# Second layer of a two-layer block on one Trainium2 core: score products of a head pair as two 64-row tiles, one exponential and one maximum for the pair, one miscellaneous PSUM bank

## The reference

```
q, k, v = x@Wq+bq, x@Wk+bk, x@Wv+bv        # q, k rotated (RoPE)
attn = softmax(q k^T / sqrt(8))            # 1024 x 1024 per head
x1 = layernorm(x + (attn v) @ Wo + bo)
comb = top-2 of softmax(x1 @ Wg), renormalised          # (1024, 8)
y[e] = gelu(x1 @ W1[e] + b1[e]) @ W2[e] + b2[e]         # all 8 experts
out = layernorm(x1 + sum_e comb[e] * y[e])
```

## Time and profile before

| | |
|---|---|
| median of 3 runs | 3107.3 us (3100.91 to 3108.63) |
| the profiled execution, its span | 3107.4 us |
| PE / DVE / ACT / POOL busy | 1506.1 / 2382.8 / 1370.3 / 173.1 us |
| layer 1 and its norms | 0 to about 1582 us |
| prologue of layer 2 | about 1582 to 1654 us |
| from V of the first pass to V of the next | 222.0 us |
| two full passes (V to V) | 711.1 us |
| tail (last values product to the end) | about 172 us |

### The profile page before, as it was taken

How to read it: one execution, slowest core, us unless ns; L and a number is a source line. 1 busy time by engine, 2 the same in 40 slices (tenths; PEclk the granted TensorE clock), 3 DMA queues, 4 the chain that set the end, 5 groups by cost and what they waited for, 6 DMA issues and landing times. The chain is left out here.

```text
span 3107.4 us, 48199 instructions
## 1 busy us (share of the span) xinstructions
PE 1506.1 (48%) x7936; PEld 733.5 (24%) x8061; DVE 2382.8 (77%) x15872; ACT 1370.3 (44%) x3634; POOL 173.1 (6%) x259
## 2 busy tenths in 40 slices
PE   2001010010100101001029998999889998999697
PEld 1000000000000000000012223444345442445264
DVE  6898988989889898898948886777566765676623
ACT  1233333333333333333524666556665666566532
POOL 3000000000000000000100200110002000110000
PEclk8555555555555555555558999999999999999999
DMA  4000000000000000000061111020200201010100
GB/s 105 1 1 1 1 1 1 1 1 1 1 1 1 1 1 1 1 1 1 2 138 20 52 29 25 1 63 8 43 1 1 63 17 33 1 52 18 25 1 7
DMA packets 59835, 56.63 MB, mean 18 GB/s; under 512 B 6602, under 2 KB 43124, under 8 KB 59488
## 3 DMA queue, kind: packets, MB, share of 16 engines
q1 hardware_dynamic: 59488, 53.20, 7.2%
HBM read 29.98 MB, written 22.54 MB: 17 GB/s over the span
## 5 line engine op out<-in xcount | busy, mean ns | idle before, releaser
L1026 DVE TENSOR_REDUCE nm_half<-s 128x1 f32<-128x512 f32 x1088 | 700.8, 685 | 246.7 <-PE s L1203 208.7
L197 ACT ACTIVATE ex<-row,nmax 128x65 f32<-128x65 f32 x960 | 335.9, 350 | 1005.5 <-DVE nmax L299 856.9
L951 ACT ACTIVATE pt<-s 128x512 f32<-128x512 f32 x1024 | 567.1, 596 | 415.2 <-PE s L1213 402.6
L257 DVE SCALAR_TENSOR_TENSOR junk<-ex,tab 128x65 f32<-128x65 f32 x2850 | 619.6, 218 | 3.4
L360 PE MATMUL p_s<-tab,bdg 128*128 128x32 f32 x120 | 31.9, 406 | 842.6 <-DVE tab L262 842.6
L1213 PE MATMUL s<-qs,ks 128*128 128x512 bf16 x949 | 361.8, 388 | 76.2 <-ACT pt L951 60.7
L1203 PE MATMUL s<-ks,qs 128*128 128x512 bf16 x1038 | 374.1, 390 | 28.7 <-DMA qs<-zeros 19.8
L262 DVE TENSOR_TENSOR tab<-raw,rz 128x1 f32<-128x1 f32 (+1 forms) x1890 | 286.4, 152 | 3.5
L1178 PE MATMUL p_o<-pt,va 128*9 128x512 f32 x2048 | 272.1, 604 | 3.4 <-ACT pt L951 1.3
L1239 PEld LDWEIGHTS bank<-w_W,hid 128*128 128x128 f32 x2048 | 257.8, 192 | 44.2 <-ACT hid L956 13.9
L1239 PE MATMUL bank<-w_W,hid 128*128 128x128 f32 x2048 | 262.9, 276 | 6.1 <-ACT hid L956 6.1
(11 more groups left out here) (178 smaller groups left out, 1461.9 us busy)
## 6 DMA issues: line engine op xcount, KB each, us to landing
parts_dram<-parts SPq DMA_DIRECT2D x60, 256.0 KB, 3.6
qs<-parts_dram SPq DMA_DIRECT2D x38, 192.0 KB
ks<-parts_dram SPq DMA_DIRECT2D x38, 192.0 KB
h_dram<-f SPq DMA_DIRECT2D x20, 128.0 KB, 2.6
hq<-h_dram SPq DMA_DIRECT2D x5, 512.0 KB, 5.2
x<-in_x SPq DMA_DIRECT2D x4, 512.0 KB, 8.6
w_W<-in_W SPq DMA_DIRECT2D x1, 2048.0 KB
w_W<-in_W SPq DMA_DIRECT2D x8, 256.0 KB
```

The lines of the kernel that those rows point to most:

```text
L197: nc.scalar.activation(ex[:, r % 2, :], row[:, r % 2, 1:], ACT.Exp, bias=nmax[:, r % 2:r % 2 + 1], accum_out=z[:, r % 2:r % 2 + 1]).then_i ...
L257: nc.vector.scalar_tensor_tensor(junk[:, g, :], ex[:, k, :], 1.0, tab[:, g, r:r + ROW], ALU.mult, ALU.mult, accum_out=raw[:, g:g + 1]).the ...
L951: nc.scalar.activation(pt[:, i % 4, tokens(t)], s2[t][:, :], ACT.Exp, scale=SCALE).then_inc(s_exp, 1)
L1026: nc.vector.reduce_max(nm_half[:, t, head // 2 % 2, head % 2, q:q + 1], s1[k % 3][:, :], AX.X, negate=True).then_inc(s_max, 1)
```

## The change

The diff's effect, step by step:

- `ks` holds both heads of a pair, one in rows 0 to 23 and one in rows 64 to 87, as `qs` did. Steps A and B are for the pair: two products, on rows 0.. and 64.. of the array, into two neighbouring banks, then **one** maximum (128 x 2 x 512) or **one** exponential (128 x 2 x 512). 128 A and 128 B in a pass.
- PSUM: `s1` is two double banks (it was three single ones), `s2` is one double bank (it was two single ones): a B waits for the whole exponential of the B before. `misc` is one bank (there were two). In the tail the experts use the four banks of `s1` in turn, in the prologue the two of `s2`.
- Y: four tiles fill one bank; DVE multiplies the 128 x 512 block by `comb` into `part`, and POOL adds it to `acc`. Experts are walked by halves of the tokens: four HID, four Y, four HID, four Y.
- The order: in place of blocks of HID, a stream of HID and Y steps is dealt into slots, one after each `B A` group, one after PV, one more in every second unit.
- The clears of `ks`, `qs`, `zeros` are gone, and with them the DMAs of `zeros` in ST (6 DMAs become 4). The first pass starts after the maxima of one head pair (it was three heads). In the tail GB, GC, CT and B2 stand ahead of the first HID.

```diff
-AFTER = {... (7, 0): [("ADD",)], (7, 1): [("LNS", 1)], ...}
-EXPERTS = {1: (0,), 2: (1,), 3: (2, 3), 4: (4,), 5: (5, 6), 6: (7,)}
-FIRST_READY, READY = 3, 4
+RINGS = {"early": 2, "main": 1, "late": 4}
+FIRST_READY, READY = 1, 2
+def expert_steps():
+    for e in range(E):
+        for half in range(2):
+            for f in range(FC):
+                yield "HID", e, FC * half + f
+            for q in range(4):
+                yield "Y", e, 4 * half + q
...
+    def slot(begun):
+        in_group = begun and stream and stream[0][0] == "Y" and stream[0][2] % 4
+        while due and not in_group:
+            x = due.pop(0)
+            yield x
+            if x == ("B2", 1):
+                weighed.append(x)
+            if bank_uses(x):
+                return
+        if begun and stream and (weighed or stream[0][0] == "HID"):
+            yield stream.pop(0)
+
+    for u in range(HP * QT):
+        hp, kt = divmod(u, QT)
+        begun = u >= QT
+        more = 3 if not moe and u < 2 * QT else 2
...
+        for t in range(2):
+            yield "B", hp, kt, t
+            yield from maxima(more - 1 if t == 0 else 1)
+            yield from slot(begun)
+        if u:
+            yield ("PV", *divmod(u - 1, QT))
...
+        yield from slot(begun)
+        if kt % 2 and begun:
+            yield from slot(begun)
...
-        s1 = [ps(f"s1{i}", [P, HALF]) for i in range(3)]
-        s2 = [ps(f"s2{i}", [P, HALF]) for i in range(2)]
-        banks = [ps(f"bank{i}", [P, 512]) for i in range(2)]
+        s1 = [ps(f"s1{t}", [P, 2, HALF]) for t in range(2)]
+        s2 = ps("s2", [P, 2, HALF])
+        misc = ps("misc", [P, 512])
...
# ScalarE, step B
-                    nc.scalar.activation(pt[:, i % 4, tokens(t)], s2[t][:, :], ACT.Exp,
+                    nc.scalar.activation(pt[:, kt % 2, :, tokens(t)], s2[:, :, :], ACT.Exp,
                                          scale=SCALE).then_inc(s_exp, 1)
# VectorE, steps A and Y
-                    nc.vector.reduce_max(nm_half[:, t, head // 2 % 2, head % 2, q:q + 1], s1[k % 3][:, :], AX.X,
-                                         negate=True).then_inc(s_max, 1)
+                    nc.vector.reduce_max(nm_half[:, t, hp % 2, :, q], s1[t][:, :, :], AX.X, negate=True)\
+                        .then_inc(s_max, 1)
-                    nc.vector.scalar_tensor_tensor(acc[:, q, :], bank[:, 0:D], comb[:, q, e:e + 1], acc[:, q, :],
-                                                   ALU.mult, ALU.add).then_inc(free, 1)
+                    if e:
+                        dve.wait_ge(s_weighed, 2 * E * (s - 1) + 2 * e + half - 1)
+                    nc.vector.tensor_tensor(part[:, half, :, :], bank.rearrange("p (q d) -> p q d", q=4),
+                                            comb[:, 4 * half:4 * half + 4, e:e + 1].broadcast_to((P, 4, D)),
+                                            ALU.mult).then_inc(free, 1)
# TensorE, step B
-                    if not (zeroth and m < 2):
-                        pe.wait_ge(s_exp, 256 * s + m - 1)
-                    nc.tensor.matmul(s2[t][:, :], ks[:, head, tile(kt)], qs[:, hp, tokens(t)], start=True,
-                                     stop=True).then_inc(s_s2, 1)
+                    if not (zeroth and hp == 0 and kt == 0 and t == 0):
+                        pe.wait_ge(s_exp, 128 * s + 16 * hp + 2 * kt + t)
+                    for par in range(2):
+                        rows = slice(64 * par, 64 * par + M_ROW + 2)
+                        ins = nc.tensor.matmul(s2[:, par, :], ks[rows, hp, tile(kt)], qs[rows, hp, tokens(t)],
+                                               start=True, stop=True)
+                    ins.then_inc(s_s2, 1)
```

More of the change, by code:

```diff
@@ L577, with bank_uses, turned @@
-EXPERTS = {1: (0,), 2: (1,), 3: (2, 3), 4: (4,), 5: (5, 6), 6: (7,)}
-FIRST_READY, READY = 3, 4
-def in_turn(first, end):
-    steps = [("A", h, q, t) for h in range(first, end) for q in range(QT) for t in range(2)]
-    return [(*x, k) for k, x in enumerate(steps)]
+             "HT": 1, "QK": 1, "PRE": 1}
+RINGS = {"early": 2, "main": 1, "late": 4}
+def bank_uses(x):
+    return 0 if x[0] == "Y" and x[2] % 4 != 3 else BANK_USES.get(x[0], 0)
+def turned(k):
+    return [("QK", k, t, i) for t in range(2) for i in range(2)]
@@ L605, in order @@
                 yield name, t
[L606 to L618, removed]
+        for name in ("GA", "GE", "GB", "GC"):
+            yield name,
+        for name in ("CT", "B2"):
+            for t in range(2):
+                yield name, t
+        yield from expert_steps()
         yield "ADD",
@@ L635, in maxima @@
             yield x
[L636 to L683, removed]
-            if i % 2:
-                yield from maxima(due)
-            if i == 1 and not hp:
-                yield "V", 0
-                yield "V", 1
-            if i == 1 and (hp or moe):
-                yield "OC", hp - 1
-            if i == 3 and (hp or moe):
-                yield "OT", hp - 1
-            yield from AHEAD.get((hp, i), ())
-            if moe:
-                yield from AFTER.get((hp, i), ())
@@ L699, in order @@
+    assert not halves and not stream
+    due += waiting
+    yield from due
     if moe:
         yield "OUT",
-PROLOGUE = ([("PRE",), ("HQ",), ("HT", 0), ("HT", 1), ("QK", 0, 0), ("QK", 0, 1), ("PO", 0), ("QK", 1, 0),
-             ("QK", 1, 1), ("PO", 1)] + [("ST", g, 1) for g in range(4)]
-            + in_turn(0, FIRST_READY)[:4 * QT] + [("MN", 0), ("MT", 0)]
-            + in_turn(0, FIRST_READY)[4 * QT:])
-ST_DMAS = 6
+PROLOGUE = ([("PRE",), ("HQ",), ("HT", 0), ("HT", 1)] + turned(0) + [("PO", 0)] + turned(1) + [("PO", 1)]
+            + [("ST", g, 1) for g in range(4)] + in_turn(0, FIRST_READY) + [("MN", 0), ("MT", 0)])
@@ L1194, in step @@
                 elif name == "A":
[L1195 to L1204 removed]
+                    hp, q, t = x[1:]
```

274 lines of the change are left out of this document (149 added, 125 removed).

## The result

The changed kernel took 3469.0 us (median of four runs, 3461.9 to 3479.1), the kernel before in the same comparison 3105.9: a ratio of 1.118, interval 1.116 to 1.120. The prediction had the sign and 3224 us, in a range that ended at 3340; the loss is three times as large as forecast.

The account below looks back on a forecast made before the run. PE bounds the kernel before; after the change, ACT's 291 us of work plus waits make a full pass 399 us against 355.5. Sum: 3107 + 130 - 8 - 5 - 6 + 6 = 3224 us, range 3135 to 3340.

Parts of the forecast that it names:

- 108 us of counted waits: Full pass: ACT's waits counted by place, 26 + 42 + 20 + 20 us, on top of 291 us of work.
- the Y stretch: Four Y of a half expert: PE about 6 us, ACT 3.3, so ACT waits 2.6 x 16 = 42 us a pass.
- The part that the prediction laid out step by step: 11 units from expert 3's first HID through half of expert 5: 90 us for 5 half experts, ACT working 72.
- a gelu behind a gelu: Full pass: with one bank the next HID starts when the gelu ends; 24 places, 26 us of ACT waits.
- The ends of a pass: Units without expert work, 8 at the start and 12 at the end: 3.0 us each, ACT waiting 1.0 x 20.
- 64 more loads: Full pass: gelus singly between exponentials make 86 table loads for 22, 82 us more of ACT work.
- rival 1: Row tiles do not overlap, each pair costs 0.43 us: +28 a full pass, +35 in the first, 3344; chance 0.10.
- Rival 2: TensorE's clock falls to 0.50 for a third of the time: +40 us a full pass, 3344; chance 0.13.
- sign of being wrong: Full passes in the profile after: a granted clock under 0.9 would show the prediction wrong.
- Start and prologue: Before the first pass: clears gone, layer 1 about -8 us; maxima of one pair and fewer DMAs, -5.
- First pass: 16 units with three maxima at 3.5 us, 48 at 3.0, 16 us for V, HT, QK: 216 against 222, -6.
- Tail: After the passes: HIDs no longer cover the choice of experts, +5 us; last addition through POOL, +1.

Follow-up runs that it names:

- loads gone: Changed kernel with Identity in the gelu's place, so nearly all table loads go; 3201.8 us.
- clock at 0.94: Changed kernel with each pair of A products issued three times into the same banks; 3525.6 us.
- full rows: Changed kernel with both products of a pair over 128 rows with zero-padded stacks, clears and zeros back; 3495.7 us, ratio 1.126.
- four HID and three banks: Changed kernel with full-row products, four HID in a slot, three misc banks and one s1 pair; 3364.2 us, ratio 1.083.
- second s2 pair: Changed kernel with two pairs of s2 banks in turn, paid for with one s1 pair; 3552.7 us, ratio 1.147.
- three banks: Changed kernel with three misc banks and one s1 pair in place of one misc bank and two s1 pairs; 3514.3 us.
- 131 with four HID: Changed kernel with three misc banks, one s1 pair and the four HID of a half expert in one slot; 3299.2 us.
- two runs without gelus: Identity in the gelu's place, in the changed kernel and in the kernel before; 3201.8 and 3083.1 us.
- clears early: Kernel before with POOL's clears moved to the start of POOL's work; 3104.3 us, ratio 0.9991.

## Why the forecast was right in its sign and wrong in its size

**The failed step: the waits of ACT in a full pass**, "108 us of counted waits", measured 183 to 187. Three times 75 are 225 of the 245 us that the forecast is short.

By place, in the first full pass: ACT idles 22 us ahead of the first HID, 132 from there to the last Y and 29 behind it. The prediction had 68 for the stretch with experts and 40 for the rest, so 64 of the 75 us lie in the stretch with experts. The term that is most wrong is the Y stretch: from the last gelu of a half expert to the first of the next ACT idles 3.7 to 13.4 us, 89.5 in 15 places, where 42 were counted for 16.

The part that the prediction laid out step by step, from the first HID of expert 3 to the end of the first half of expert 5, took 103.5 us for 90, with 73.8 of work for 72; so even there the layout was 12 us of waits short, and carrying it to all 16 halves missed that the first five leave ACT idle 5.6 to 13.4 us each, all but one over 7.

Sorted by what stands ahead on ACT, in the same pass (idle times of its timeline added up): a gelu behind a gelu 34.7 us in 24 places, where the prediction had 26 in 24; an exponential behind an exponential 111.3 in 76 places; all other places, at the seams between gelus, exponentials and copies, 36. The prediction had 82 for the last two.

The waits of exponentials stay at 121 to 145 us a pass in every variant of the changed kernel: loads gone (122), clock at 0.94 (127), full rows (121; 145 with four HID and three banks), second s2 pair (130), three banks (143; 131 with four HID). None of the single buffers or prices sets them alone; what these variants have in common is the order, in which PE takes B, A, PV, HID and Y in turn and each waits for another engine. That it is the order is argued from this, not shown by a run that changes it and gains. Two parts are plain in the trace:

- The Y stretch shown above: 4.5 us of waits where 2.6 were counted, of which some 1.9 are the first Y and PV at half clock (1.92 and 1.87 us for 0.89 and 0.98). In the five stretches of this pass that ran at full clock ACT still idles 3.7 us or more.
- The ends of a pass, which I had at 3.0 us a unit and 25 us for norms, V and QK. The blocks of eight units before the first and behind the last expert work, by windows of the changed kernel:

```profile
1869.52:1907.91 38.39, 30.36 (x191) 11.07 (x189) 29.89 (x55) 22.21 (x25) 0.00 (x0) 0.83 0.16 28
...
2296.71:2339.24 42.53, 24.52 (x132) 4.12 (x130) 31.66 (x61) 22.10 (x22) 0.00 (x0) 0.75 0.05 15
```

4.8 and more than 5 us a unit, with ACT working 22 us of each. In a norm, maxima stand behind its scaling and gain on DVE, A behind the maxima and B behind A:

```profile
2307.86 0.92 DVE L1003 BATCH_NORM_AGGREGATE mv<-stats 128x2 f32<-128x6 f32 x8
2308.70 4.62 DVE L1033 TENSOR_REDUCE nm_half<-s 128x2 f32<-128x1024 f32 x4
2309.99 0.61 PE L1212 MATMUL s<-ks,qs 48*128 48x512 bf16 x2 [3.28 <-DVE nm_half L1033]
2310.39 0.64 PE L1223 MATMUL s<-qs,ks 50*128 50x512 bf16 x2
2311.07 1.02 ACT L959 ACTIVATE pt<-s 128x1024 f32<-128x1024 f32 x1 [3.30 <-PE s L1223]
```

**Right: the work.** 64 more loads a pass at 1283 ns without a drain, the wide exponential, ACT's 291 us, and that ACT and its waits, not PE, set a full pass. The two runs without gelus put 83 us a pass on the loads, what the sum had (82); since the clock rose and the waits grew (185 to 200 us a pass) with the same edit, the agreement is in part luck.

**Right: the row tiles overlap** (rival 1 out), by 0.22 us for a pair. Missed was the price of entering and leaving them, 0.30 us a round trip, which I had set at 0.1. In the changed kernel they gain 30 us in the first pass and lose 8 to 10 in each of two full ones.

**Rival 2, the clock,** came true in the rows: 0.86 and 0.85, under the 0.9 that the prediction had named as a sign of being wrong. It was priced at 40 us a pass for half clock in a third of the time. The half clock held for 136 us of the first full pass, 29% of it, and in 63 of these PE was busy while ACT stood idle (71 in the second pass). At full clock that work would take half as long: an estimate of up to 31 to 35 us a pass, near the rival's price and part of the 75. The pair of Y stretches above, 1.43 us for one fall of the clock, points the same way. No run measures it by itself. With A three times (0.94) and with full rows (0.95) a pass is unchanged or 8 to 10 us shorter, but both raise the clock by giving PE more to do, and what the clock gave back there paid for the added work. By this estimate some 40 of the 75 us would be left at full clock.

**The small parts.** Start and prologue -14.1 for -13, right. First pass -1.2 for -6. Tail +14.6 for +6: the choice of experts left open is as forecast, but the first four HID take 5.64 us where the next four take 3.60 (granted clock 0.65 there, then 1.00), and a half expert takes 8.11 us (3334.45 to 3342.56) where the sum had 7.85: 16 times 0.26 is 4.2 us. CT and B2, in front of the first HID now and at half clock, take 5.5 us for 3.0 at full clock. Two slips of the prediction's sums change little: 325 less 56 us of PE work is 269, not 255, and waits of 80 us a pass give 3140, not 3135.

## What to carry to other kernels

Count table loads from the order, and give a group of gelus more than one bank before making it (three for four here): each edit alone gave 15 to 17 us a pass, both together 87. Where no engine is full and each waits for another in turn, lay out the ends of a pass and its norms step by step too, not only its middle; a sum of waits by kinds of place was 40% short here. Read the granted clock of the stretches, too: an engine that is no longer the bound can still lengthen the waits of the one that is. Tile a product by rows only where two of them run at once. No version here with the reference's outputs beats the kernel before by more than can be told; the nearest has its clears early (0.9991).

## What the runs showed of the hardware

- A way from full f32 products into a row-tiled bf16 product and back cost 0.30 us (1.59 against 1.29 for the same three steps). The Trainium skill's page TensorEngine Tiling (Array Packing), Key Properties, says that a change of tiling mode drains TensorE, and gives no price; the trace agrees that there is one.
- The granted clock fell to 0.58 in stretches in which PE's rows were 92 to 100% busy with single row-tiled products among the others (27.76 of 30 us, 19.95 of 20), and was 1.00 in comparable stretches of the kernel before over full rows (0.99 over its full passes). Whether the half rows or the steps between tilings do it is not shown.
- A clear of 128x8192 bf16 on POOL held a 128x32 instruction of DVE for 6.19 us, and did not lengthen its batch statistics (6.28 us with the clear beside it, 6.29 without).
- A fall of the granted clock to a mean of 0.79 in a Y stretch lengthened ACT's wait there from 2.36 to 3.79 us, with the same steps in both.
- The same unchanged products ahead of layer 1's loop took 1.13 us and came 2.24 apart in some runs, and 2.07 us and 3.60 apart in others, with a granted clock of 1.00 in the rows of both. The first two products are 3.60 apart in every trace, the long kind.
